# Splitting the tail of a per-edge tensor product: GpSimd halves four product tiles a block, VectorE sums them in one instruction, ScalarE scales features

## The reference

```python
x0 = x[src][:, :16]                         # 16 scalars of the source node
x1 = x[src][:, 16:].reshape(-1, 16, 3)      # 16 vectors
sh0, sh1 = edge_attr_4[:, 0], edge_attr_4[:, 1:4]
w00, w01, w10, w11 = (silu(edge_attr_32 @ w1 + b1) @ w2 + b2).reshape(-1, 4, 16, 16)  # per edge
out0 = a * (einsum('eu,e,euw->ew', x0, sh0, w00) + einsum('eui,ei,euw->ew', x1, sh1, w11) / 3**.5)
out1 = a * (einsum('eu,ei,euw->ewi', x0, sh1, w01) + einsum('eui,e,euw->ewi', x1, sh0, w10)) / 3**.5
agg  = segment_sum(concat([out0, out1]), dst)
```

## Time and profile before

| | |
|---|---|
| median of 3 runs | 22464.6 us (22409.09 to 22469.32) |
| the profiled execution | 22394.77 us |
| its span in the profile | 22392.9 us |
| busy VectorE, GpSimd, TensorE, ScalarE, share of the span | 69%, 58%, 45%, 12% |
| first layer, first to last block's comparison matrix | 3574.8 to 10046.8 us |

### The profile page before, as it was taken

The page is one execution under the profiler, slowest core; times in us unless marked ns, Lnnn a source line. Parts: engine busy times, 40 slices in busy tenths (PEclk is TensorE's granted clock), DMA queues, the critical chain, the costliest instruction groups (busy, mean ns, idle before and its releaser), DMA issues. The chain is left out here.

```text
span 22392.9 us, 208316 instructions
## 1 busy us (share of the span) xinstructions
PE 9998.2 (45%) x47565; PEld 6760.8 (30%) x47566; DVE 15533.6 (69%) x25706; ACT 2711.3 (12%) x6738; POOL 12929.4 (58%) x12678
## 2 busy tenths in 40 slices
PE   0033334555555555555666633333243443334333
PEld 0033332222222222222222333332243343234333
DVE  8744446999999999997666511112578777577777
ACT  0011110000000000000000000000133233223332
POOL 0088886666666666655666426665455553455553
PEclk9999997555555555557888755555555555555555
DMA  4033331111111111121111201112422222222222
GB/s 182 16 70 68 70 70 37 25 25 25 24 24 24 24 24 24 24 22 24 24 24 24 18 13 23 23 23 23 66 61 59 64 62 46 61 61 63 58 62 49
DMA packets 1151518, 957.54 MB, mean 43 GB/s; under 512 B 803963, under 2 KB 920315, under 8 KB 1150739
## 3 DMA queue, kind: packets, MB, share of 16 engines
q0 software_dynamic: 419904, 437.84, 11.4%
q1 hardware_dynamic: 730960, 512.22, 8.9%
HBM read 734.68 MB, written 210.63 MB: 42 GB/s over the span
## 5 line engine op out<-in xcount | busy, mean ns | idle before, releaser
L1461 POOL DMA_INDIRECT tail<-ball,h_idx x3328 | 3449.7, 1037 | 3131.9 <-issue 1400.1
L737 PE MATMUL p_rad<-w_stack,hid_t 99*128 99x512 bf16 (+1 forms) x6656 | 2879.5, 589 | 2470.7 <-DVEq L828 1094.6
L1497 PE MATMUL h_sum<-head,h_hot 128*128 128x64 f32 x6656 | 1429.6, 414 | 3369.5 <-ACT head L1542 2051.0
L810 DVE TENSOR_REDUCE red<-prod 128x96 f32<-128x1536 f32 x1664 | 2896.4, 1741 | 3.5
L1497 PEld LDWEIGHTS h_sum<-head,h_hot 128*128 128x128 f32 x6656 | 1396.4, 324 | 3396.1 <-issue 3396.0
L693 POOL DMA_INDIRECT rec_b<-l_rcb x1600 | 2065.7, 1291 | 570.8 <-issue 514.5
L1109 POOL DMA_INDIRECT l_xg<-h_tab,l_idx x1664 | 1572.3, 945 | 1285.8 <-issue 614.3
L338 POOL DMA_INDIRECT rec_a<-rec,slot x1600 | 1986.8, 1242 | 517.5 <-issue 503.5
L933 POOL DMA_INDIRECT l_xg<-x_tab,l_idx x1664 | 1572.4, 945 | 1148.5 <-issue 841.0
L949 PE MATMUL l_sum<-outer,l_hot 128*128 128x512 f32 x3328 | 1681.4, 669 | 972.1 <-DVEq L994 896.2
L737 PEld LDWEIGHTS p_rad<-w_stack,hid_t 99*128 99x128 bf16 (+1 forms) x6656 | 777.3, 131 | 4221.8 <-issue 4170.5
(11 more groups left out here) (368 smaller groups left out, 17982.3 us busy)
## 6 DMA issues: line engine op xcount, KB each, us to landing
hot_t<-rows_l SPq DMA_DIRECT2D x208, 512.0 KB
rec_a<-fill SPq DMA_DIRECT2D x128, 728.0 KB, 19.5
l_rec<-rec_a SPq DMA_DIRECT2D x104, 896.0 KB, 4.9
rhot_t<-rows_r SPq DMA_DIRECT2D x208, 384.0 KB
tail<-ball,h_idx POOLq DMA_INDIRECT x3328
t<-in_type SPq DMA_DIRECT2D x100, 500.0 KB
l_xg<-in_x,l_idx POOLq DMA_INDIRECT x1664
l_xg<-x_tab,l_idx POOLq DMA_INDIRECT x1664
```

The lines of the kernel that those rows point to most:

```text
L737: ins = pe.matmul(p_rad[j % 3][:, h * 512:(h + 1) * 512], hid_t[j // 4 % 2][0:K3 + 3 * (1 - i), j % 4, i, :], w_stack[i][0:K3 + 3 * (1 - i ...
L810: ch.step(dve.tensor_reduce(red[:, j, :], prod[j % 3][:, :, :], AX, ALU.add))
L1461: pool.indirect_dma_start(tg[q][:, j, :], None, table[:, :], bass.IndirectOffsetOnAxis(ap=idx[q][:, j:j + 1], axis=0)).then_inc(gathered[q ...
L1497: ins = pe.matmul(p_sum[u % 2][:, j % BT // 2, :], hot[j // HP8 % 3][:, j % HP8, :], hg[:, j, 0:D], start=(j % 2 == 0), stop=(j % 2 == 1))
```

## The change

All of it is in `product_phase`.

- Four tiles of a block, 1 to 4, get a product buffer of their own, `dealt`. VectorE no longer reduces them one by one.
- When VectorE has made the products of tile 5, it raises `dealt_done`. GpSimd (`halves`) then adds, for each of the four tiles, the upper eight of every sixteen numbers onto the lower eight, in place, and raises `halved`.
- At the block's end VectorE waits for `halved` and sums the eights of all four tiles in one instruction, ahead of the reduction of tile 15.
- ScalarE (`scaled_features`) takes over x0·sh0, the copy of x0 and x1·sh0: one copy and 32 scalings a block; VectorE waits for it (`scaled`) beside `feat_done`. GpSimd keeps the three instructions that make the sh1 row.
- On GpSimd the order of a block becomes: features of block b+1, halves of block b, scatters of block b+1.
- In the tiles whose reduction is gone, the addition into the node sums stands between the products and the wait.

SP's queue and TensorE's are as they were.

```diff
+            def halves(b):
+                hold(pool, turn, dealt_done, b + 1)
+                for k in range(DEALT):
+                    o = dealt[:, k, :, :]
+                    ch.step(pool.tensor_tensor(o[:, :, 0:HALF], o[:, :, 0:HALF], o[:, :, HALF:MUL], ALU.add))
+                ch.sync()
+                pool.sem_inc(halved, 1)
+                ch.restart()
...
+            with pool.Fori(0, SB // 2 - 1) as it:
+                features(it, 1)
+                halves(it * 2)
+                scatters(it, 1)
+                features(it + 1, 0)
+                halves(it * 2 + 1)
+                scatters(it + 1, 0)
...
+                act.activation(f[:, :, 2, :], xg[q][:, :, 0:MUL], ACT.Copy)
+                for j in range(BT):
+                    sh0 = r[:, j, R_SH:R_SH + 1]
+                    act.activation(f[:, j, 0, :], xg[q][:, j, 0:MUL], ACT.Copy, scale=sh0)
+                    ins = act.activation(f[:, j, 3:6, :], x1[:, j, :, :], ACT.Copy, scale=sh0)
+                ins.then_inc(scaled, 1)
...
-                f, o = feat[q], prod[j % 3]
+                f, o = feat[q], dealt[:, j - 1, :, :] if 1 <= j <= DEALT else prod[j % 3]
...
                 for j in range(2, EARLY):
                     products(b, q, j)
-                    reduce(j - 1, 2)
-                    dve.wait_ge(chain_s, ch.n - 1)
+                    mark = ch.n
+                    if j - 1 > DEALT:
+                        reduce(j - 1, 2)
+                    else:
+                        dve.wait_ge(chain_s, mark - 2)
+                        add(j - 2)
+                    dve.wait_ge(chain_s, mark)
                     dve.sem_inc(tile_done, 1)
-                    add(j - 2)
+                    if j - 1 > DEALT:
+                        add(j - 2)
+                    elif j - 1 == DEALT:
+                        dve.sem_inc(dealt_done, 1)
...
-                reduce(BT - 1, 0)
+                dve.wait_ge(halved, b + 1)
+                ch.step(dve.tensor_reduce(red[:, 1:1 + DEALT, :], dealt[:, :, :, 0:HALF], AX, ALU.add))
+                reduce(BT - 1, 1)
```

More of the change, by code:

```diff
@@ L620, in product_phase @@
         prod = [sb(f"prod{k}", [P, 96, MUL]) for k in range(3)]
+        HALF = MUL // 2
+        DEALT = 4
+        dealt = sb("prod_dealt", [P, DEALT, 96, MUL])
         red = sb("red", [P, BT, 96])
@@ L628, in product_phase @@
         rcb_in, rcb_sent = [sem(f"rcb_in{q}") for q in range(2)], [sem(f"rcb_sent{q}") for q in range(2)]
-        turned, kept, rad_done, tile_done, msg_done, sum_done, rec_used, w_done, turn, chain_s, pc, feat_done, w_split, w_stacked, added = (
+        (turned, kept, rad_done, tile_done, msg_done, sum_done, rec_used, w_done, turn, chain_s, pc, feat_done, w_split, w_stacked, added,
+         scaled, dealt_done, halved) = (
             sem("l0_" + n) for n in ("turned", "kept", "rad_done", "tile_done", "msg_done", "sum_done",
-                                     "rec_used", "w_done", "turn", "chain", "pool_chain", "feat_done", "w_split", "w_stacked", "added"))
+                                     "rec_used", "w_done", "turn", "chain", "pool_chain", "feat_done", "w_split", "w_stacked", "added",
+                                     "scaled", "dealt_done", "halved"))
         block = ctx.enter_context(nc.Block())
@@ L662, in _, with features @@
             ch = Chain(pool, pc)
-            def one(it, q, scattering):
+            def features(it, q):
                 b = it * 2 + q
@@ L675, in one @@
                 f, r = feat[q], rec[q]
-                x0 = xg[q][:, :, 0:MUL]
                 x1 = xg[q][:, :, MUL:D].rearrange("p t (u i) -> p t u i", i=3)
-                sh0, sh1 = r[:, :, R_SH:R_SH + 1], r[:, :, R_SH + 1:R_SH + SH]
+                sh1 = r[:, :, R_SH + 1:R_SH + SH]
                 v4 = vec[:, :, :].rearrange("p t (u i) -> p t u i", i=3)
[L680 to L685, removed]
+                ch.do(pool.tensor_tensor(v4, x1, bc(sh1.unsqueeze(2), [P, BT, MUL, 3]), ALU.mult))
                 ch.do(pool.tensor_tensor(f[:, :, 1, :], v4[:, :, :, 0], v4[:, :, :, 1], ALU.add))
@@ L689, in one, with scatters @@
                 ch.restart()
[L690 to L699, removed]
+            def halves(b):
[6 more added lines that the diff above has]
+                ch.restart()
+            def scatters(it, q):
+                hold(pool, turn, rcb_in[q], it * 16 + 16)
+                for j in range(BT):
+                    pool.indirect_dma_start(rec_b[:, :], bass.IndirectOffsetOnAxis(ap=rcb[q][:, j, 3:4].bitcast(U32), axis=0),
+                                            rcb[q][:, j, :], None).then_inc(rcb_sent[q], 16)
+            features(0, 0)
+            scatters(0, 0)
+            with pool.Fori(0, SB // 2 - 1) as it:
[5 more added lines that the diff above has]
+                scatters(it + 1, 0)
+            features(SB // 2 - 1, 1)
+            halves(SB - 2)
+            scatters(SB // 2 - 1, 1)
             with pool.Fori(SB // 2, NB // 2) as it:
                 for q in range(2):
-                    one(it, q, False)
+                    features(it, q)
+                    halves(it * 2 + (q - 1))
+            halves(NB - 1)
             for q in range(2):
@@ L708, in _, with scaled_features, body @@
             act.sem_inc(kept, SEED)
-            with act.Fori(0, NB) as b:
+            def scaled_features(it, q):
+                hold(act, turn, rec_in[q], it * 16 + 16)
+                hold(act, turn, gathered[q], it * (16 * BT) + 16 * BT)
+                f, r = feat[q], rec[q]
+                x1 = xg[q][:, :, MUL:D].rearrange("p t (u i) -> p t i u", i=3)
+                act.activation(f[:, :, 2, :], xg[q][:, :, 0:MUL], ACT.Copy)
+                for j in range(BT):
+                    sh0 = r[:, j, R_SH:R_SH + 1]
+                    act.activation(f[:, j, 0, :], xg[q][:, j, 0:MUL], ACT.Copy, scale=sh0)
+                    ins = act.activation(f[:, j, 3:6, :], x1[:, j, :, :], ACT.Copy, scale=sh0)
+                ins.then_inc(scaled, 1)
+            def body(b, q, it, left):
                 for k in range(BT // 4):
@@ L713, in _ @@
                     act.activation(hid_t[k % 2][0:K3, :, :, :], p_turn[:, :, :, :], ACT.Copy).then_inc(kept, 1)
+                if left:
+                    scaled_features(it + q, 1 - q)
+            scaled_features(0, 0)
+            all_blocks(act, NB, body)
         @block.tensor
@@ L816, in first_tiles @@
                 dve.wait_ge(feat_done, b + 1)
+                dve.wait_ge(scaled, b + 1)
                 products(b, q, 0)
```

## The result

The changed kernel takes 22803.9 us (median of four runs, 22753.4 to 22858.55) where the kernel before took 22452.9 in the runs beside it: a ratio of 1.0156, 95% interval 1.0138 to 1.0174. The forecast was 22805, within 22590 to 23030. The profiled execution took 22753.4 us, 359 more than that of before.

The account below looks back on a forecast made before the run. GpSimd's serial loop was to become the bound: 60.2 - 3.0 + 6.5 + 0.8 + 1.6 = 66.1 us a block, 349 us over 97 blocks, ends -18 and +9, together +340 on 22464.6: 22805 us, range 22590 to 23030.

Parts of the forecast that it names:

- GpSimd's loop, 60.2 us undisturbed, and no room in it: GpSimd's serial round through SP's waits and loads takes 60.2 us a block undisturbed, against VectorE's 62.5.
- Features off GpSimd, -3.0: On GpSimd, the feature instructions moved to ScalarE save 3.0 us a block.
- Half-additions, 6.5: On GpSimd, four in-place additions at 1.62 us each add 6.5 us a block, ends 5.8 and 7.8.
- The second handover, 0.8: On GpSimd, another increment, clear and wait add 0.8 us a block, ends 0.6 and 1.1.
- Stall in the scatters, 1.6: GpSimd's scatters lose 1.6 us a block beside VectorE's messages and comparison matrix, ends 1.0 and 2.3.
- The sign that was named, one scatter of 2 to 3 us a block: In GpSimd's timeline, one scatter a block taking 2 to 3 us would show the forecast right.
- VectorE alone, 58.9: VectorE's own work falls by 3.6 us, to 58.9 us a block.
- ScalarE: 33 small instructions at 0.256 us, 8.4 us a block, stay hidden unless each took 0.6 us.
- The ends: The first block loses about 9 us uncovered; the last five, not waiting for scatters, gain 18 us.
- TensorE keeps up: A tile's matmuls take 1.86 us, against 2.05 us for a tile without reduction on VectorE.
- The 66.1 us a block: GpSimd's loop after the change: 64.5 us undisturbed plus 1.6 us of scatter stall.
- The rival with GpSimd's third of free time as usable room: GpSimd, 68% busy, has room, so VectorE's saving is the result: 22094 us; chance 0.09.

Follow-up runs that it names:

- Experiment 2: The kernel before, with SP issuing the next block's record load before waiting for the current block's scatters to land: 22316.59 us, ratio 0.9996.
- experiment 1: The changed kernel, with SP issuing the next block's record load before waiting for the current block's scatters to land: 21918.56 us, ratio 0.9813.
- 3: The changed kernel without the four half-additions on GpSimd, handover kept, the long reduction summing only the lower eights: 21960.37 us, ratio 0.983.
- 8: The changed kernel with the half-additions ahead of the next block's features on GpSimd in place of behind them: 22093.68 us, ratio 0.9845.
- experiment 6: The changed kernel with all feature rows back on GpSimd, so half-additions without ScalarE's help: 23073.91 us, ratio 1.0287.
- experiment 4: The changed kernel with half-additions written to a buffer of their own, which the long reduction reads, not in place: 22668.37 us, ratio 1.0146.

## Why the prediction was right

- **GpSimd's loop, 60.2 us undisturbed, and no room in it.** Right, and it decided all. Experiment 2 shows that it stood below VectorE's pace before, experiments 1, 3 and 8 that it stood above it afterwards. The records are waited for as long as forecast, some 7 us.
- **Features off GpSimd, -3.0.** Measured 3.08 left of 6.03, and 69.30 - 66.35 = 2.95 in experiment 6.
- **Half-additions, 6.5.** Measured 7.03. The size came within the ends, but the reason was wrong: the 0.15 us of L687 over L686 was read as the price of being in place, and experiment 4 shows no such price. They measured 1.79 long, 1.745 from start to start. The estimate of 1.69 by the Trainium skill's page GPSIMD Engine Reference, "Elementwise — side-by-side cycle accounting", was nearer to that than the 1.62 of the sum.
- **The second handover, 0.8.** Measured 0.41 + 1.14 - 1.13 = 0.42. Too high by 0.4, which takes back most of the 0.5 by which the additions were too low.
- **Stall in the scatters, 1.6.** Measured 24.88 - 23.43 = 1.45. Of the scatters shown the one at 5069.83 bears the most, 1.89 us, beside the comparison matrix. The sign that was named, one scatter of 2 to 3 us a block, did not show: another one of the block takes 1.81, and none of all 1600 over 1.90. The rule in the Trainium skill, SBUF — State Buffer, "Who interferes with whom", as the prediction took it (the loser blocks fully), would have allowed 4.7. The same section infers that a two-input instruction like these leaves GpSimd free to prepare a DMA, by which nothing would be lost; the trace lies between the two.
- **VectorE alone, 58.9.** Measured 58.4 by its wait, and 58.71 in experiment 1, where that wait is gone. The long reduction takes 3.353 us, forecast 3.35. The 0.5 us that VectorE saved beyond the forecast is a term that the prediction left out: before, the messages often ran beside GpSimd's last feature instructions, now beside scatters. From 4000 to 9700 us the four instructions from the first message to the matrix took 5.10 us together on average, and take 4.67 now. The one with the largest change follows, before (5000 to 5500 us) and after (4000 to 9700 us; count, then busy us and mean ns). Before, from 4000 to 9700 us, it took 1.52 us in the 49 blocks where it ran beside feature instructions, and 0.95 in the other 42.

```profile
L843 DVE TENSOR_TENSOR msg<-red,l_rec 128x768 f32<-128x768 f32 x8 | 10.0, 1246 | 0.0
```

```profile
L893 DVE TENSOR_TENSOR msg<-red,l_rec 128x768 f32<-128x768 f32 x86 | 81.8, 951 | 0.0
```

- **ScalarE.** Its 33 instructions are over well before VectorE can start on them: VectorE's wait before the products is as forecast, none for `scaled`. The estimate of 8.4 us for them was near: 5049.98 to 5057.55, 7.6 us.
- **The ends.** The first block lost 9.9 us (100.2 against 90.3 between the first two matrices), forecast 9. The last five were to gain 18 and lost 4.7: 58.7 and 60.0 us as forecast, then three of 66.4. This term had the wrong sign. In those three VectorE waits 9.0 us a block for TensorE's tiles (1.2 and 0.8 in the two before them), which the prediction had excluded ("TensorE keeps up"); in the rest of the layer that held.

The sum comes to 3.81 us a block over 97 blocks, 370, with the ends 385, beside 383 for the stage; the forecast had 349 and -9. So the sum is 45 us over the 340 forecast: 21 in the blocks, 24 in the ends. The profiled executions differ by only 359, as the time outside the stage, which the change doesn't touch, came out 25 us shorter (15921 and 15896), and the medians differ by 351. That the measured 22803.9 stands 1 us from the forecast 22805 is luck. The 66.1 us a block owe part of their closeness to errors that cancel, too: the handover's takes back most of the additions'. The rival with GpSimd's third of free time as usable room fell: at 69% busy GpSimd's round was full.

## What to carry to other kernels

Busy time doesn't say how much room an engine has. Add up one round of its loop from the timeline, with the waits that its own work brings about (here: scatters landing, SP's issue, the record load), and compare that sum with the bound engine's period before giving it work. If the round is full, look in it for an idle stretch that the new work can stand in, or move what triggers the load: the same change cost 1.6% with the additions behind the features, and gained 1.6% with them in the idle time, and 1.9% with the load issued earlier.

## What the runs showed of the hardware that was not expected

Where GpSimd runs early and its gathers fall beside the first tiles of a block, VectorE waits for tiles that TensorE seems to have finished long before. From experiment 2, VectorE's timeline, then TensorE's:

```profile
5008.06 0.21 DVE L857 TENSOR_TENSOR acc_nodes<-acc_nodes,l_sum 128x64 f32 x1
5010.64 0.96 DVE L803 TENSOR_TENSOR prod<-p_rad,feat 128x768 f32<-128x768 f32 x1 [2.38 <-remote]
```

```profile
4999.64 1.58 PE L739 MATMUL p_rad<-w_stack,hid_t 99*128 99x512 bf16 x4 [2.23 <-DVEq L830]
5003.16 1.86 PE L739 MATMUL p_rad<-w_stack,hid_t 99*128 99x512 bf16 x4 [1.94 <-issue]
...
5006.68 1.86 PE L739 MATMUL p_rad<-w_stack,hid_t 99*128 99x512 bf16 x4 [0.80 <-issue]
```

VectorE's second line is tile 7, TensorE's lines are tiles 7, 8 and 9. Tile 7's four matmuls are recorded from 4999.64 for 1.58 us, and VectorE got leave at 5010.64. In that trace 35 such waits of over 0.4 us, of together 71 us from 4000 to 9700 us, stand at tile 7, each beginning 0.2 to 0.8 us after GpSimd has issued the last of a block's gathers; the kernel before has none there. The ends of matmuls are modelled in these profiles, so TensorE might really have been late. But the trace also keeps the times of semaphore increments: those of tiles 7, 8 and 9 stand at 5010.62, 5010.68 and 5010.83, though the matmuls started 3.5 us apart, and ScalarE's next copy was released in between, at 5010.77. Tile 9's four matmuls, which start at least 0.38 us apart, cannot have run in the last 0.15 us, so its increment at least was late. From 4000 to 9700 us, increments of neighbouring tiles stand under 0.4 us apart 107 times in experiment 2, and never in the kernel before or the changed one, whose last three blocks then have five. What holds them back was not tried, and stays open.

It is why early loading didn't shorten the block before (62.89 us against 62.54). The waits at tiles 6 and 7 add 0.82 us a block; the messages and the matrix, with nothing of GpSimd's beside them, take 4.63 us in place of 5.10. The last three blocks of the changed kernel show waits of the same kind, here at tiles 5 and 6 of one, beside gathers that go out from 10302.88 to 10322.66:

```profile
10315.03 0.96 DVE L840 TENSOR_TENSOR prod<-p_rad,feat 128x768 f32<-128x768 f32 x1 [3.44 <-remote]
...
10320.69 0.96 DVE L840 TENSOR_TENSOR prod<-p_rad,feat 128x768 f32<-128x768 f32 x1 [3.71 <-remote]
```
